# First fold of the score weights: full-height products of an even and an odd head stand ahead of both heads' 64-row products

## What is computed

```
x = x + tanh(g_xattn[0]) * L0_xattn(ctx, ctx, masks, layernorm(x), Wq, bq, Wk, bk)   # softmax weights (256x256) themselves
x = x + tanh(g_ffn[0])   * L0_ffn(layernorm(x), ...)      # 8 experts of 176, top 2, bfloat16, and a shared expert
x = x + tanh(g_xattn[1]) * L1_xattn(layernorm(x), ctx, ...)
x = x + tanh(g_ffn[1])   * L1_ffn(layernorm(x), ...)      # 8 experts of 256, top 2, float32
```

```
q_hk = (hidden_q @ Wq.T).reshape(b, s, 16, 128)
q_big = einsum('bshk,hkq->bshq', q_hk, w_kc_q)            # 192 per head
kv_rope = rope(kv_c)
q_r = einsum('bshq,hqr->bhsr', q_big, W_qr)               # 64 per head
k_r = einsum('bld,hdr->bhlr', kv_rope, W_kr)
scores = einsum('bhsr,bhlr->bhsl', q_r, k_r)
```

## Time and profile before

| | |
|---|---|
| runs, us | 473.12, 474.0, 474.25 |
| profiled execution, span from first to last instruction | 472.4 us |
| TensorE (PE) matmuls, busy | 401.0 us, 85% |
| VectorE (DVE), busy | 325.9 us, 69% |
| ScalarE (ACT), busy | 235.2 us, 50% |
| first fold's products (lines 1240, 1241), busy | 7.9 and 7.9 us, 32 recorded matmuls each |

### The profile page before, as it was taken

The page is one execution under the profiler, slowest core; times in us unless marked ns, Lnnn a source line. Parts: engine busy times, 40 slices in busy tenths (PEclk is TensorE's granted clock), DMA queues, the critical chain, the costliest instruction groups (busy, mean ns, idle before and its releaser), DMA issues. The chain is left out here.

```text
span 472.4 us, 7935 instructions
## 1 busy us (share of the span) xinstructions
PE 401.0 (85%) x2691; PEld 332.9 (70%) x2691; DVE 325.9 (69%) x772; ACT 235.2 (50%) x515; POOL 135.7 (29%) x140
## 2 busy tenths in 40 slices
PE   1669896758899988998988898778998799999996
PEld 0335594437689777888778796668897677778885
DVE  0889849454899458998559995668772357555885
ACT  1013667326369546497465695553365344444331
POOL 4815100004301137102046011244268910001730
PEclk9999978878579999999999999998999899999999
DMA  6995700093011001010011010030354422211320
GB/s 157 291 328 186 101 2 0 9 311 102 1 24 24 3 0 46 1 26 22 1 25 24 2 45 1 2 90 24 89 186 150 145 80 89 90 46 46 111 92 22
DMA packets 30743, 35.37 MB, mean 75 GB/s; under 512 B 5712, under 2 KB 25792, under 8 KB 30448
## 3 DMA queue, kind: packets, MB, share of 16 engines
q1 hardware_dynamic: 26304, 28.11, 19.7%
q0 software_dynamic: 4400, 6.75, 6.4%
HBM read 25.61 MB, written 7.60 MB: 70 GB/s over the span
## 5 line engine op out<-in xcount | busy, mean ns | idle before, releaser
L1753 DVE RECIPROCAL egh<-egh 128x256 bf16<-128x256 bf16 x44 | 76.5, 1740 | 2.0 <-ACT egh L920 2.0
L1388 PE MATMUL bank<-kv,probs 128*128 128x128 f32 x512 | 67.5, 275 | 3.4 <-ACT negmT L981 2.9
L1388 PEld LDWEIGHTS bank<-kv,probs 128*128 128x128 f32 x512 | 62.5, 192 | 4.1 <-issue 4.1
L1008 ACT ACTIVATE probs<-bank 128x512 f32<-128x512 f32 x64 | 36.9, 587 | 16.9 <-PE bank L1368 16.9
L1837 DVE TENSOR_REDUCE negm<-bank 128x2 f32<-128x512 f32 x64 | 41.3, 686 | 4.0 <-PE bank L1347 3.6
L1347 PE MATMUL bank<-Kh,Qs 128*128 128x256 f32 x128 | 32.7, 351 | 9.7 <-DVE negm L1837 4.8
L1367 PE MATMUL bank<-Qs,Kh 128*128 128x256 f32 x128 | 39.4, 329 | 0.0
L733 POOL TENSOR_SCALAR veps<-mv 128x2 f32<-128x2 f32 x12 | 2.7, 226 | 126.1 <-DVE mv L1584 126.1
L916 ACT ACTIVATE gu_all<-bank 128x512 bf16<-128x512 f32 x44 | 26.0, 590 | 24.0 <-PE bank L1171 23.8
L1550 PEld LDWEIGHTS bank<-W,hTs 128*128 128x128 f32 x210 | 28.1, 189 | 13.3 <-DVE hTs L1991 7.6
L1550 PE MATMUL bank<-W,hTs 128*128 128x256 f32 (+1 forms) x210 | 32.9, 293 | 3.8 <-DVE hTs L1991 2.6
(11 more groups left out here) (205 smaller groups left out, 890.7 us busy)
## 6 DMA issues: line engine op xcount, KB each, us to landing
Qm<-Qs SPq DMA_DIRECT2D x32, 128.0 KB
xs<-f3A SPq DMA_DIRECT2D x1, 2432.0 KB, 9.9
Qm<-xs SPq DMA_DIRECT2D x19, 128.0 KB, 2.1
ys<-y SPq DMA_DIRECT2D x19, 128.0 KB, 2.0
w_q<-in_wq SPq DMA_DIRECT2D x2, 1024.0 KB, 17.6
w_o<-in_woT SPq DMA_DIRECT2D x1, 2048.0 KB, 11.4
w_in<-in_L_ffn_Wg SPq DMA_DIRECT2D x8, 256.0 KB, 5.0
w_in<-in_L_ffn_Wu SPq DMA_DIRECT2D x8, 256.0 KB, 3.0
```

The lines of the kernel that those rows point to most:

```text
L1008: done(act.activation(flat(pT[:, n % 3]), bank1(b, FILL_ST + h)[:], ACT.Exp), "p_ready")
L1388: ins = pe.matmul(bank_v(b, h // 2)[:, at:at + P], pT[:, n % 3, lt, t * P:(t + 1) * P], kv_all[:, frm:frm + P], start=(lt == 0), stop=(lt ...
L1753: done(dve.reciprocal(eg[:, j], eg[:, j]), "e1")
```

## The change

In `of_r(q)` the loop over four heads, each with its full-height product and then its 64-row product, becomes a loop over two pairs of heads. For a pair, the full-height products of the even and of the odd head are issued first, and then the 64-row products of both. The same products are computed with the same operands, into the same parts of bank 4, and the semaphore is still incremented by the last of them.

```
-                    for h in range(4 * q, 4 * q + 4):
-                        o = bank[4][half(h), h // 2 % 4 * KD:(h // 2 % 4 + 1) * KD]
-                        pe.matmul(o, w_qra[:, h], w_kqa[:, h], start=True, stop=False)
-                        ins = pe.matmul(o, w_qrb[half(h), h // 2], w_kqb[half(h), h // 2], start=False, stop=True)
+                    def o(h):
+                        return bank[4][half(h), h // 2 % 4 * KD:(h // 2 % 4 + 1) * KD]
+
+                    for pr in range(2 * q, 2 * q + 2):
+                        for h in (2 * pr, 2 * pr + 1):
+                            pe.matmul(o(h), w_qra[:, h], w_kqa[:, h], start=True, stop=False)
+                        for h in (2 * pr, 2 * pr + 1):
+                            ins = pe.matmul(o(h), w_qrb[half(h), pr], w_kqb[half(h), pr], start=False, stop=True)
                     if q % 2:
                         done(ins, "a_fold")
```

## The result

The changed kernel took 473.06 us (median of 17 runs, 471.06 to 473.69) against 474.0 us (17 runs beside them): ratio 0.9972 with a 95% interval of 0.9960 to 0.9983, that is 1.3 us less (0.8 to 1.9). The ratios of this document are estimated from all runs, not from the two medians, which lie 0.9 us apart here. In a second comparison, at the end of the series, it was 472.33 against 474.14 us, ratio 0.9964 (0.9941 to 0.9987), that is 1.7 us less (0.6 to 2.8). The forecast was 472.2 us, 1.8 less, with a range of 470.4 to 474.4. Runs more than 1.5% above the fastest of the same kernel are left out of its ratio; that concerns two runs of one kernel (e9) alone.

What follows compares the result with a forecast made beforehand. TensorE, busy 85%, leads but bounds only one stretch between 33 and 85 us, otherwise holding others up by 1.5 and 0.3 us. Of 6.8 us saved, 1.53 + 0.28 = 1.8 count: 474.0 - 1.8 = 472.2 us, range 470.4 to 474.4.

Steps and rivals of the forecast that it cites:

- The pace: In `of_r`, a pair costs one product's step; a call takes 1.44 us instead of 2.89, or 2.47 instead of 4.94.
- The path: From `of_r(0)` to `lgm`: bank 4's copy 1.88 us earlier, VectorE's reciprocal 1.53, `lgm` 1.8 earlier with the third-fill wait gone.
- What was late next: After bank 4's copy and the first fill's exponentials, VectorE's own work until 48.49 us limits the gain to 1.53 us there.
- the two new idle times: TensorE stands 1.7 us at bank 4 before `of_r(2)`, and some 4.8 us instead of 1.67 ahead of `turn_hs`.
- The forecast is insensitive to whether the pairs overlap.: Without overlap TensorE saves 1.9 us before bank 4's copy, just the 1.88 us that ScalarE can use.
- the fewer changes of shape: Eight in each `of_r` become four, saving 0.7 us in each fast call and 1.2 in the slow one.
- this rival at the idle ahead of `turn_hs`: Longer idle there leaves half clock behind it, costing 3.2 us less the 1.8 gained: 475.4 us; chance 0.10.
- The size: Whole kernel: 1.8 us gained, the median falling from 474.0 to 472.2 us; chance 0.50.
- the scatter behind 85 us, which it cost at nothing: From 85 us to the end, everything was taken to move with compute, with no fixed point stopping the gain.
- rival 1: Gain partly lost behind 66 us, in the many short waits from 101 to 136 us: 0.8 us left, 473.2 us; chance 0.27.

Runs made afterwards that it cites:

- e9: e1 again, for a second profile: pair order in `of_r(0)` and `of_r(1)` alone; 476.95 us, ratio 1.0030 to the kernel before.
- e8: e1 with a second bank (7) for `of_r(2)` and `of_r(3)`, so TensorE doesn't wait for the copy; 473.15 us, ratio 0.9982 to before.
- e2: Kernel before with the pair order in `of_r(2)` and `of_r(3)` alone, behind the copy; 474.47 us, ratio 0.9999 to before.
- e3: Products of a call reordered so same-shape neighbours use the same array half and can't run at once; 473.35 us, ratio 0.9966 to before.
- e12: The changed kernel itself again, for a second profile and comparison; 472.33 against 474.14 us, ratio 0.9964.
- e4: The changed kernel with the router and `turn_hs` two fills later (LATE = 5 in place of 3); 471.22 us, ratio 0.9930 to before.
- e1: Kernel before with the pair order in `of_r(0)` and `of_r(1)` alone, ahead of the copy; 476.71 us against 474.74, ratio 1.0031.

## Why the prediction was right

- **The pace.** Forecast: a pair costs one product's step, 0.361 and 0.617 us; `of_r(0)` ends at 35.47, `of_r(1)` at 43.9. Measured: 0.37 and 0.62, 35.52 and 43.93. The Trainium skill (TensorE: Matmul & The Clock Gate, Part 3, The mechanism) says that a weight load overlaps running matmuls only where the row groups differ. The trace doesn't agree: the full-height pair uses the same rows, and its four weight loads and four matmuls take 0.37 us. The Trainium skill (TensorEngine Tiling (Array Packing), Gotcha 1: PSUM Pressure) says that different row tiles can't access the same PSUM bank at once. The trace doesn't agree for halves of one bank that lie on different partitions: the 64-row pair writes bank 4 from both row halves in one step of 0.37 us.
- **The path.** Forecast: copy at 45.99, reciprocals at 48.49, `lgm` at 56.15, `turn_hs` at 56.47. Measured: 45.91, 48.43, 55.95, 56.27. What was late next was named each time, and the two new idle times too (1.7 and 4.8; measured 1.68 and 4.59). e8 and e2 show by runs that the calls ahead of the copy carry the gain and those behind it none.
- **"The forecast is insensitive to whether the pairs overlap."** Half right. The prediction valued the fewer changes of shape at 0.7 us a fast call and 1.2 in the slow one, from the 0.17 us of idle ahead of a weight load. The change still has these 0.17 us ahead of each of its four weight loads, but by e3 a neighbour without a change of shape saves only 0.14 us (0.36 against 0.22) and at half clock 0.19 (0.62 against 0.43). Without overlap TensorE would thus save 4 x 0.14 + 4 x 0.19 = 1.3 us ahead of the copy (an estimate) and not 1.9, and the copy would have come later than it did. In runs e3 gained as much as the change, in its profile 1.32 against 2.19 us.
- **The clock.** The prediction had this rival at the idle ahead of `turn_hs`, and e2 shows that this one is harmless; it cost the idle at bank 4 at nothing beyond the wait itself. e9, e12 and e4 show half clock behind it. For the change that did no harm on the path, since its pairs at half speed still end ahead of `lgm`: the saving behind the copy, worth nothing at full clock, is the cover at half clock. Without it (e1) the kernel was 1.5 us slower than before, though only the loss of the gain is seen in rows. That the change brought its own cover was luck: the prediction didn't reckon with it.
- **The size.** Forecast 1.8, profile 2.0 at `lgm` and 2.2 to 2.5 behind, runs 1.3 (0.8 to 1.9) and 1.7 (0.6 to 2.8). Both intervals hold 1.8, so the runs don't show a term to be mis-sized. What the prediction lacked is the scatter behind 85 us, which it cost at nothing: the second profile of the change was 1.3 us ahead of the first at Mq (62.68 against 63.94) and ended 4.0 behind it, so 5.3 us come and go behind 66 us, three times the gain. Whether part of the gain is regularly lost there (rival 1) stays open: for before there is one profile.

## What to carry

Work taken from an engine counts only up to the next hand-over; follow each hand-over in the profile until some engine is late by its own work, and that gives the gain, here 1.8 of 6.8 us. What is saved beyond it becomes idle time, and on TensorE idle time isn't free: behind 2.46 to 2.90 us of it the clock was at half in three profiles here, so ask whether the work that follows still ends in time at half speed. One profile is one draw: compare it with the spread of times before a term of 1 or 2 us is read from it.

## What the hardware showed that I had not expected

TensorE can be at work for long and stay at half clock: in e9 it had no pause from 46.58 to 66 us, mostly with the fold's products, and its granted clock was 0.50 from 48 to 63 us. Where the clock falls differs between executions of one kernel, and so does the time: e1 and e9, the same kernel, took 471.8 to 479.42 us. The cover of the change doesn't end this. Its first 17 runs lay within 2.6 us (471.06 to 473.69), but the 12 of e12 within 4.9 (471.18 to 476.05). And two products in different halves of the array started within the same step, 0.37 us for both, although they share a bank.
